# Linear result writes, gathers by batch and a deeper pipeline in the third expert layer of a four-layer attention and expert stack

## The chip, the cores and the metric

The kernel runs on one core of one Trainium2 chip. The metric is the time of one execution on the device, in microseconds (us), as the median of three runs. PE is the matrix engine (TensorE) and PEld its weight loads, DVE is VectorE, ACT is ScalarE, POOL is GpSimd, and SP is SyncE, which here only issues transfers and keeps them in order. HBM is the chip's memory off the core; SBUF and PSUM are the two memories on it.

## The reference, cut to what matters

`x` has 4 batches of 512 tokens of 128 numbers, `ctx` 4 batches of 154 tokens. Four layers follow each other, each with a cross-attention and a layer of 8 experts. The change lies in the experts of layer 2 (counted from 0, so the third) and in the attentions of layers 2 and 3:

```python
x = x + _L2_xattn_ref(_layernorm(x), ctx, ...)      # 16 heads of 64, softmax over 154 keys
x = x + _L2_ffn_ref(_layernorm(x), wg, w1, w2)
x = x + _L3_xattn_ref(_layernorm(x), ctx, ctx, ...) # 16 heads of 64
x = x + _L3_ffn_ref(_layernorm(x), ...)

def _L2_ffn_ref(x, wg, w1, w2):                     # w1 8x128x256, w2 8x256x128
    gate_logits = xt @ wg
    top_vals, top_idx = jax.lax.top_k(gate_logits, TOP_K)          # TOP_K = 2
    weights = jax.nn.softmax(top_vals, axis=-1)
    combine = zeros((T, E)).at[arange(T)[:, None], top_idx].add(weights)
    h = jax.nn.gelu(jnp.einsum('td,edf->etf', xt, w1), approximate=False)
    y = jnp.einsum('etf,efd->etd', h, w2)
    out = jnp.einsum('te,etd->td', combine, y)
```

Every token goes to two experts, so each expert layer has 4096 rows to compute, and a token's result is the sum of two weighted rows.

## The kernel before

**Experts of layers 2 and 3 (`region`).** POOL scatters the 4096 normalised rows, each with its weight and its target, by indirect DMA into `xq_d` in HBM, so that the rows of an expert stand together (`slot_q` holds the place of every row, `scatter_rows`, L903). The rows are then worked in NRUN = 23 runs, 16 of 256 rows and 7 of 128, which make 39 blocks of 128 rows. Per run SP loads the expert's two weight matrices (`weights(k)`, L721 and L722, into one of NQ = 4 slots) and SP or ACT loads the rows (`rows(k)`, L730 and L1269, into one of 8 slots). PE turns the rows (`columns`, L2857), ACT copies them (`xc_q`), PE makes the hidden layer (`hidden`, L2869), ACT applies the gelu, PE multiplies by the second matrix (`down`, L2882), and DVE scales each row by its gate weight into one of NY = 6 result tiles `yq` (`weigh`, L2030). PE's order is hidden(k+1), columns(k+2), down(k). DVE also works out for each block where its rows belong (`targets`, L2022), and POOL scatters the block to those rows of `yq_d` in HBM by indirect DMA (L922), 39 times. When all have landed, SP issues eight linear loads (L756) of the two halves into `acc` and `y_other`. DVE adds them to `x_tok` (L1778, L1780).

**Attentions of layers 2 and 3.** The heads are taken in 4 groups of 4, and the work in 16 stages, one for a group and a batch. A stage has 8 steps m, one for a pair of heads and a tile of 128 tokens: PE makes the scores (L2777 to L2779), DVE their maxima (L2278), ACT the exponentials (L1323), DVE the reciprocal of the sum, POOL scales (`normalise`, L1085 and L1086), and PE turns the result and multiplies by the values one stage later. A group has 13 preparations (`prep`: products of the weights with the context, copied by ACT and DVE). Those of groups 0 and 1 stand ahead of stage 0, those of group 2 in stages 4 to 7, of group 3 in stages 8 to 11. The order of stages is written out in `ORDER`: group 0 for batches 0 to 3, then group 1 for batches 0 to 3, then a mix. Before a batch's first stage its layer norm has to be ready: DVE adds the results to `x_tok` and takes the statistics (L1728, L1731, L1736), POOL raises to the power -1/2 (`rstd`, L892), DVE normalises (L1745), PE turns (`turned_x`), ACT copies, and POOL takes the low part of the split (`low_x`, L1071). In the order before, DVE does batches 0 and 1 and most of batch 2 ahead of its first maxima.

The engines run each its own list in order; semaphores tie them. The name of a loop's step is the order of the code: nothing is scheduled by a planner except the positions in tables such as `ORDER`.

Of the kernel before, what the change touches and what calls it, by code (L numbers as in the profile page):

```python
# [6 lines left out]
def xattn_moe_stack(nc, t, out):  # L7
# [55 lines left out]
    NQ, NX, NY = 4, 8, 6  # L63
# [9 lines left out]
    PRIOR = (None, None, 7, 8)  # L73
    SPOT = (0, 2, 3, 4, 5, 6, 7, 8, 9, 10, 11, 12, 13)
# [4 lines left out]
    BEHIND = {(0, "A"): [("x", 1)], (0, "C"): [("x", 2)], (2, "A"): [("x", 3)], (13, "A"): [("f", 0)], (14, "A"): [("f", 1)], (14, "D"): [("t", 0)], (15, "A"): [("lg", 0)], (15, "D"): [("t", 1)]}  # L79
# [8 lines left out]
    def ring(l):  # L88
# [70 lines left out]
    with ExitStack() as ctx:  # L159
# [229 lines left out]
        w1_q = [over(f"w1_q{u}", [P, 4 * P], F32, w_q_at[u])[0] for u in range(NQ)]  # L389
        w2_q = [over(f"w2_q{u}", [P, 4, D], F32, w_q_at[u] + 2048)[0] for u in range(NQ)]  # L390
        xq = [over(f"xq{u}", [P, HALVES, XC], F32, q_at + 1056 * u)[0] for u in range(NX)]
        yq = [over(f"yq{u}", [P, HALVES, D], F32, pt_at + 10240 + 1024 * u)[0] for u in range(NY)]
        xc_q = [over(f"xc_q{u}", [P, RUN], F32, pt_at + 8192 + 1024 * u)[0] for u in range(2)]
        h_q = [over(f"h_q{u}", [P, 4, RUN], F32, pt_at + 4096 * u)[0] for u in range(2)]
# [259 lines left out]
        def _(sp):  # L654
# [56 lines left out]
            def region(l):  # L711
# [3 lines left out]
                def weights(k):  # L715
# [3 lines left out]
                    if k >= NQ:  # L719
                        sp.wait_ge(q_yp, run(l, k - NQ) + 1)  # L720
# [2937 lines left out]
```

## Time and profile before

| | |
|---|---|
| median of three runs | 1168.32 us (1166.42, 1168.32, 1173.46) |
| profiled execution, first to last instruction | 1219.8 us |
| mean granted clock of PE in it | 0.930 of full speed |
| busy: PE, DVE, ACT, POOL | 86%, 59%, 53%, 47% |
| third expert layer, first turn of rows to SP's first result load | 784.9 to 853.2 us |
| first scores of the attentions of layers 2 and 3 | 528.3 and 872.0 us |

The profiled execution has no time of its own other than its span, which is 51.5 us longer than the median. So the places in the trace tell what waits for what, and a time that is read off it may be up to some per cent longer than in the runs that are timed. A line number such as L922 is one of the kernel before.

### The profile page before, as it was taken

To read this page: it belongs to the slowest core of one execution; us is meant where nothing else is said; L and a number is where in the kernel's file an instruction comes from. 1 tells how busy PE (TensorE), PEld (TensorE's weight loads), DVE (VectorE), ACT (ScalarE), POOL (GpSimd) and SP (SyncE) were. 2 spreads that over 40 slices of the span, in tenths; PEclk is the share of its full clock that TensorE was granted. 3 is DMA by queue.
4 is the path that set the end of the run, shared out by engine and by line. 5 is a ranking of instruction groups with operands and counts; after the bars stand their busy time and mean duration, and the time that the engine had idled before them with its cause. 6 is when DMAs were issued, how large, how long until landed. Compare 5 with 4: busy or idle time off the path is not lost.

```text
span 1219.8 us, 22199 instructions
## 1 busy us (share of the span) xinstructions
PE 1054.1 (86%) x6815; PEld 797.4 (65%) x6815; DVE 717.3 (59%) x2444; ACT 643.9 (53%) x2117; POOL 571.5 (47%) x926
## 2 busy tenths in 40 slices
PE   4988999758889998979999987777799999977994
PEld 3865788735555667856767665566566776654994
DVE  5575354476776771386767784322876776852444
ACT  2244323357778723358778862222387888731321
POOL 5223655451000152566555656366375555655452
PEclk9987999989999988889999997697899999986997
DMA  2003556599600124110000001364300000014665
GB/s 63 13 27 112 161 165 208 163 156 385 237 1 1 36 68 137 54 30 19 1 19 19 1 5 43 85 187 121 87 19 1 2 1 1 2 33 129 200 208 173
DMA packets 116005, 102.87 MB, mean 84 GB/s; under 512 B 18027, under 2 KB 97571, under 8 KB 115888
## 3 DMA queue, kind: packets, MB, share of 16 engines
q1 hardware_dynamic: 105280, 82.71, 23.3%
q0 software_dynamic: 8448, 17.20, 4.2%
q10 hardware_dynamic: 2160, 1.53, 0.5%
q8 instruction: 57, 0.93, 0.3%
q14 instruction: 60, 0.49, 0.1%
HBM read 65.04 MB, written 36.36 MB: 83 GB/s over the span
## 4 chain that ended last, share of the span: by engine, by line
PE 61%; DVE 16%; issue 6%; ACT 5%; POOL 4%; DMA 4%; another core or an unknown queue 3%; SPq 2%; DVEq 0%; ACTq 0%; POOLq 0%
PE ps L2973 4%; PE ps L2777 4%; PE ps L2869 4%; PE ps L2882 4%; PE ps L2779 4%; PE ps L2778 4%; PE ps L2987 3%; PE ps L3515 3%; PE ps L3519 3%; PE ps L3168 2%; PE ps L3528 2%; PE ps L3001 2%; PE ps L3327 2%; ACT ex L1323 2%
## 5 line engine op out<-in xcount | busy, mean ns | idle before, releaser
L1323 ACT ACTIVATE ex<-ps,nmx 128x154 f32<-128x154 f32 x512 | 194.0, 391 | 75.0 <-DVE nmx L2278 73.2
L1085 POOL TENSOR_TENSOR pp<-ex,rc 128x256 f32<-128x256 f32 x256 | 157.6, 615 | 146.0 <-DVE rc L2283 145.0
L2278 DVE TENSOR_REDUCE nmx<-ps 128x2 f32<-128x308 f32 x256 | 119.6, 470 | 60.2 <-PE ps L2779 59.2
L922 POOL DMA_INDIRECT yq_d<-yq,ids_q x78 | 74.7, 957 | 79.4 <-DVE yq L2030 60.6
L2973 PEld LDWEIGHTS ps<-ident,pp 128*128 128x128 f32 x640 | 73.9, 142 | 55.5 <-POOL pp L1086 46.5
L2777 PE MATMUL ps<-kp,q_s 128*128 128x308 f32 x256 | 95.5, 373 | 15.1 <-ACT ex L1323 12.6
L1323 ACT ACTIVATION_READ_ACCUMULATOR ex<-ps,nmx 128x1 f32 x512 | 105.2, 205 | 0.0
L2973 PE MATMUL ps<-ident,pp 128*128 128x128 f32 x640 | 100.1, 280 | 2.8 <-POOL pp L1086 2.8
L1440 ACT ACTIVATE pe<-ps,nmx 128x154 f32<-128x154 f32 x256 | 84.9, 394 | 32.0 <-DVE nmx L2161 30.9
L892 POOL TENSOR_TENSOR ln_r<-ln_v,mhalf 128x4 f32<-128x4 f32 x32 | 32.7, 1021 | 105.4 <-DVE ln_v L1736 86.8
L2869 PE MATMUL ps<-xc_q,w_q 128*128 128x256 f32 (+1 forms) x276 | 63.6, 371 | 19.3 <-issue 11.5
L2778 PE MATMUL ps<-kp,q_s 128*128 128x308 f32 x256 | 79.1, 309 | 0.0
L2779 PE MATMUL ps<-kp,q_s 128*128 128x308 f32 x256 | 79.0, 309 | 0.0
L2609 DVE SCALAR_TENSOR_TENSOR h_r<-ps,bias_r,g_r 128x256 f32<-128x256 f32 (+1 forms) x92 | 34.6, 437 | 73.7 <-ACT g_r L1598 45.2
L903 POOL DMA_INDIRECT xq_d<-xe,slot_q x64 | 61.8, 965 | 33.0 <-issue 17.9
L2752 PE MATMUL ps<-ident_bf 128*128 128x512 bf16 x193 | 66.7, 497 | 6.1 <-DVE ln_v L1736 6.1
L2161 DVE TENSOR_REDUCE nmx<-ps 128x2 f32<-128x308 f32 x128 | 58.6, 474 | 21.6 <-PE ps L3155 21.2
L1086 POOL TENSOR_TENSOR pp<-ex,rc 128x52 f32<-128x52 f32 x256 | 70.9, 277 | 0.0
L2987 PE MATMUL ps<-pt_s,vv 128*64 128x512 f32 x256 | 69.0, 618 | 1.4 <-ACT pt_s L1336 1.4
L1241 ACT ACTIVATE xc_q<-ps 128x256 f32<-128x256 f32 (+1 forms) x46 | 16.0, 351 | 101.6 <-PE ps L2857 73.7
L2030 DVE TENSOR_SCALAR yq<-ps,xq 128x128 f32<-128x128 f32 x78 | 24.3, 347 | 74.9 <-PE ps L2882 48.9
L1130 POOL COPY pr<-pe 128x416 f32<-128x416 f32 x16 | 8.6, 537 | 123.7 <-ACT pe L1440 123.7
(481 smaller groups left out, 2831.6 us busy)
## 6 DMA issues: line engine op xcount, KB each, us to landing
w_r<-in_L_ffn_W SPq DMA_DIRECT2D x69, 256.0 KB
xq_d<-blankq SPq DMA_DIRECT2D x4, 4160.0 KB, 23.8
w_q<-in_L_ffn_W SPq DMA_DIRECT2D x46, 256.0 KB
w_q<-in_L_ffn_w SPq DMA_DIRECT2D x46, 128.0 KB
xq<-xq_d SPq DMA_DIRECT2D x24, 130.0 KB
w_s<-in_L_ffn_W SPq DMA_DIRECT2D x8, 256.0 KB
w_e<-in_L_ffn_W SPq DMA_DIRECT2D x8, 256.0 KB, 5.2
acc<-yq_d SPq DMA_DIRECT2D x8, 256.0 KB, 4.6
```

The source lines that it names most:

```text
L922: pool.indirect_dma_start(yq_d[:, :], bass.IndirectOffsetOnAxis(ap=ids_q[:, c:c + 1], axis=0), yq[k % NY][:, h, :], None).then_inc(q_out[k ...
L1085: pool.tensor_tensor(pp[st % 2][:, m % 4, 2 * j:2 * j + 2, :], w[:, :, 0:P], r.broadcast_to([P, 2, P]), ALU.mult)
L1086: pool.tensor_tensor(pp[st % 2][:, m % 4, 4, :].rearrange("p (h c) -> p h c", h=4)[:, 2 * j:2 * j + 2, 0:SK - P], w[:, :, P:SK], r.broadca ...
L1323: ins = act.activation(ex[:, tt % NEX, j, :], ps[:, tt % 3, j * SK:(j + 1) * SK], ACT.Exp, bias=nmx8[:, tt % 8, j:j + 1], accum_out=sm8[:, ...
L1440: ins = act.activation(pe1[st % 2][:, m % 4, m // 4 * 2 + j, 0:SK], ps[:, tt % 3, j * SK:(j + 1) * SK], ACT.Exp, bias=nmx8[:, tt % 8, j:j ...
L2278: dve.tensor_reduce(nmx8[:, tt % 8, :], ps[:, tt % 3, 0:2 * SK].rearrange("p (h s) -> p h s", h=2), AX.X, ALU.max, negate=True).then_inc(n ...
L2777: mm(bank, w[0], x[0], start=first, stop=False)
L2778: mm(bank, w[0], x[1], start=False, stop=False)
L2779: return mm(bank, w[1], x[0], start=False, stop=last)
L2869: last = mm(ps[:, k % 2 * 2 + c // 2, c % 2 * RUN:c % 2 * RUN + P * TALL[k]], w1_q[k % NQ][:, c * P:(c + 1) * P], xc_q[k % 2][:, 0:P * TAL ...
L2973: last = pe.transpose(ps[:, bank, k * P:(k + 1) * P], pp[st % 2][:, k, c, :], ident[:, :])
L2987: last = mm(ps[64 * i:64 * i + 64, 5 + j, :], vv[g % 2][:, b, 64 * h:64 * h + 64], pt_s[h][:, :], start=True, stop=False)
```

## The change

**Results.** In layer 2, POOL's 39 scatters, DVE's `targets` and the eight loads at the end are gone. SP writes each run's results as they stand, with one linear DMA (`results(k)`), to a new tensor `yl_d`, at the row where the run stands in `xq_d` (`row_y`, two small DVE operations in the table of runs). In SP's order `results(k-4)` stands behind `weights(k)`, and waits for DVE's `weigh(k-4)`. `yl_d` is filled with zeros beforehand, by two more DMAs behind the zero writes of `xq_d` in layer 1.

**Gathers.** Within the attention of layer 3 POOL gathers, with `slot_q`, the two rows of each token from `yl_d` into `acc` and `y_other`: `fetch(b, i)`, 32 indirect DMAs of 128 rows, 8 for a batch. Twelve stand ahead of the first `rstd`, two between it and `low_x(0)`, four behind that, and 14 among the 32 `normalise` of stages 0 to 3.

**Pipeline.** In layer 2 there are three hidden and three result banks instead of two, four `xc` tiles instead of two, and PE's order is hidden(k+2), columns(k+4), down(k). Weights have six slots instead of four.

**Order of the attentions of layers 2 and 3.** Groups 0 and 1 go batch by batch: (0, b0), (1, b0), (0, b1), (1, b1) and so on. Layer norm and turning of batches 1 to 3 move into stages 0 to 5, and the 26 preparations of groups 2 and 3 to stages 2 to 12. Ahead of stage 0 only batch 0 is left. In layer 3, twelve instead of eight preparations of group 1 stand ahead of batch 0's sums.

```diff
+    PREP_AT = {(2, 0): [(2, 0)], (2, 2): [(2, 1)], (3, 0): [(2, 4)], (3, 1): [(2, 5)], (3, 3): [(2, 6)], (4, 0): [(2, 7)], (5, 0): [(3, 0)],
...
-    ORDER = [(g, b) for g in range(2) for b in range(B)] + [(2, 0), (2, 1), (3, 0), (3, 1), (2, 2), (3, 2), (2, 3), (3, 3)]
+    ORDER = [(g, b) for b in range(B) for g in range(2)] + [(2, 0), (2, 1), (3, 0), (3, 1), (2, 2), (3, 2), (2, 3), (3, 3)]
...
+    FETCH_AT = {(0, 1): (2, 2), (0, 3): (2, 3), (0, 5): (2, 4), (0, 6): (2, 5), (1, 1): (2, 6), (1, 3): (2, 7), (1, 5): (3, 0), (2, 1): (3, 1), (2, 3): (3, 2),
+                (2, 5): (3, 3), (2, 6): (3, 4), (3, 1): (3, 5), (3, 3): (3, 6), (3, 5): (3, 7)}
...
+                def results(k):
+
+                    sp.wait_ge(q_y, max(run(l, k), 1))
+                    r = sp.value_load(row_y[0:1, UNIT[k]:UNIT[k] + 1])
+                    sp.wait_ge(q_y, run(l, k) + 1)
+                    sp.dma_start(yl_d[bass.ds(r, P * TALL[k]), :].rearrange("(p h) c -> p h c", h=TALL[k]), yq[k % NY][:, 0:TALL[k], :]).then_inc(q_lin[k % NY], 16)
...
-                for k in range(NQ, NRUN):
+                for k in range(4, NRUN):
                     weights(k)
...
+                    if l == 2:
+                        results(k - 4)
+                if l == 2:
+                    for k in range(NRUN - 4, NRUN):
+                        results(k)
+                    return
...
+                for h in range(2):
+                    sp.dma_start(yl_d[h * EMPTY // 2:(h + 1) * EMPTY // 2, :].rearrange("(k p) c -> p k c", p=P),
+                                 blankq[:, 0:1, 0:D].broadcast_to([P, EMPTY // (2 * P), D])).then_inc(q_init, 16)
...
-                for k in range(NRUN):
+                for k in range(NRUN if l == 3 else 0):
                     pool.wait_ge(q_y, run(l, k) + 1)
...
+                def fetch(b, i):
+
+                    c, n = i % 2, i // 2
+                    into = (acc, y_other)[c]
+                    pool.indirect_dma_start(into[:, b * S + n * D:b * S + (n + 1) * D], None, yl_d[0:EMPTY, :],
+                                            bass.IndirectOffsetOnAxis(ap=slot_q[:, b, c * TB + n:c * TB + n + 1], axis=0)).then_inc(y_row[b], 16)
...
+                if l == 3:
+                    for k in range(NRUN - NY, NRUN):
+                        pool.wait_ge(*sent(2, k))
+                    for i in range(2 * TB):
+                        fetch(0, i)
+                    for i in range(4):
+                        fetch(1, i)
                 rstd(2 * l, 0)
-                rstd(2 * l, 1)
...
                 for k in range(NRUN):
-                    if k + 1 < NRUN:
-                        hidden(k + 1)
-                    if k + 2 < NRUN:
-                        columns(k + 2)
+                    if k + ahead < NRUN:
+                        hidden(k + ahead)
+                    if k + 2 * ahead < NRUN:
+                        columns(k + 2 * ahead)
                     down(k)
```

SP's list in the third expert layer, in mid loop. Before, behind the last rows that SP loads, only weights are left (`w_q` are weight slots):

```order
245 L730 ISA
246 L730 DMA xq_213<-xq_d 128x260
247 L718 TENSOR_LOAD expert_q
248 L721 ISA
249 L721 DMA w_q_200<-in_L_ffn_w 128x256
250 L722 DMA w_q_204<-in_L_ffn_w 128x2x128
251 L718 TENSOR_LOAD expert_q
```

Now a result write stands between the weights of two runs (`w_h` are weight slots, `ids_q` holds `row_y`, `yq` are result tiles):

```order
244 L739 TENSOR_LOAD expert_q
245 L742 ISA
246 L742 DMA w_h_203<-in_L_ffn_w 128x256
247 L743 DMA w_h_213<-in_L_ffn_w 128x2x128
248 L748 TENSOR_LOAD row_q
249 L751 ISA
250 L751 DMA xq_225<-xq_d 128x260
251 L756 TENSOR_LOAD ids_q
252 L758 ISA
253 L758 DMA yl_d<-yq_227 128x256
254 L739 TENSOR_LOAD expert_q
```

Every load of weights behind the first five has moved to behind a write that waits for DVE.

POOL's list at the head of the fourth attention, before, from the last two scatters (`wo_hl` are parts of the output weights, `ln_r` is `rstd`, `q_s` is `low_x`, `pp` is `normalise`):

```order
488 L922 DMA yq_d<-yq_217,ids_q 9984x128
489 L922 DMA yq_d<-yq_218,ids_q 9984x128
490 L1024 TENSOR_TENSOR wo_hl_86<-w_raw,ones 128x256
491 L1026 TENSOR_TENSOR wo_hl_87<-w_raw,wo_hl_86 128x256
492 L892 TENSOR_TENSOR ln_r<-ln_v,mhalf 128x4 x2
493 L1071 TENSOR_TENSOR q_s<-xnT,q_s 128x512
494 L892 TENSOR_TENSOR ln_r<-ln_v,mhalf 128x4
495 L1085 TENSOR_TENSOR pp_90<-ex,rc 128x256
```

Now, from the twelfth gather on:

```order
481 L1114 DMA y_other<-yl_d,slot_q 128x128
482 L929 TENSOR_TENSOR ln_r<-ln_v,mhalf 128x4
483 L1114 DMA acc<-yl_d,slot_q 128x128
484 L1114 DMA y_other<-yl_d,slot_q 128x128
485 L1108 TENSOR_TENSOR q_s<-xnT,q_s 128x512
486 L1114 DMA acc<-yl_d,slot_q 128x128
487 L1114 DMA y_other<-yl_d,slot_q 128x128
488 L1114 DMA acc<-yl_d,slot_q 128x128
489 L1114 DMA y_other<-yl_d,slot_q 128x128
490 L1129 TENSOR_TENSOR pp_90<-ex,rc 128x256
```

The gathers stand ahead of and between the steps that lead to the first scores and the first `normalise`; the `rstd` of later batches have gone from there.

DVE's list at the same place, before, from batch 0's `rstd` result on to the first maxima `nmx` (`xn_tok` is the normalised batch, `kp` and `vr` are preparations):

```order
1176 L1745 TENSOR_SCALAR xn_tok<-x_tok,ln_mv,ln_r 128x128 x4
1177 L1778 TENSOR_TENSOR x_tok<-x_tok,y_other 128x512
1178 L1780 TENSOR_TENSOR x_tok<-x_tok,acc 128x512
1179 L1728 BN_STATS ln_st<-x_tok 128x6 x4
1180 L1731 BN_AGGR ln_mv<-ln_st 128x2 x4
1181 L1736 TENSOR_SCALAR ln_v<-ln_mv 128x4
1182 L1852 TENSOR_TENSOR kp_79<-ps,kp_78 128x308 x2
```

Now:

```order
1155 L1800 TENSOR_SCALAR xn_tok<-x_tok,ln_mv,ln_r 128x128 x4
1156 L1914 COPY vr_94<-ps 128x256
1157 L2344 TENSOR_REDUCE nmx<-ps 128x2 x2
1158 L2349 RECIPROCAL rc<-sm 128x2
1159 L1826 TENSOR_TENSOR x_tok<-x_tok,y_other 128x512
1160 L2344 TENSOR_REDUCE nmx<-ps 128x2
```

The sums and statistics of batches 1 and 2 have moved behind the first maxima, where the add (L1826) waits for batch 1's gathers.

## Rows read from the trace of the kernel before

**Rows 1.** The page, part 4: the chain that ended last, by engine.

```profile
PE 61%; DVE 16%; issue 6%; ACT 5%; POOL 4%; DMA 4%; another core or an unknown queue 3%; SPq 2%; DVEq 0%; ACTq 0%; POOLq 0%
```

**Rows 2.** Stretches: length, busy PE, PEld, DVE, ACT, POOL, clock, DMA share, GB/s.

```profile
330.00:390.00 60.00, 56.13 (x446) 35.20 (x446) 41.82 (x93) 48.16 (x133) 3.23 (x6) 1.00 0.01 2
528.30:573.40 45.10, 39.98 (x232) 28.02 (x233) 32.84 (x107) 36.30 (x148) 33.35 (x69) 0.92 0.05 13
872.00:919.00 47.00, 39.77 (x231) 27.02 (x232) 35.68 (x109) 35.21 (x148) 33.78 (x69) 0.96 0.04 13
919.00:970.00 51.00, 50.21 (x348) 36.96 (x346) 35.68 (x99) 41.03 (x161) 28.46 (x68) 1.00 0.01 2
```

**Rows 3.** Line L922 in 784.9 to 852.9; its engine's idle time (us, times).

```profile
L922 POOL DMA_INDIRECT yq_d<-yq,ids_q x39: 952/958/961, 792.0 to 850.8; - x39
...
  issue: 9.9, 31
```

**Rows 4.** Waits, 785 to 850: who, for whom, us, times, longest.

```profile
ACT xc_q L1241 <- remote: 20.2, 6, 4.8
...
DVE yq L2030 <- remote: 15.1, 4, 4.5
```

**Rows 5.** Timeline in the third expert layer: start, us, engine, line, operation.

```profile
797.80 0.33 SPq L721 DMA_DIRECT2D w_q<-in_L_ffn_w  x1
...
799.09 0.33 SPq L721 DMA_DIRECT2D w_q<-in_L_ffn_w  x1
...
800.74 0.61 DVE L2030 TENSOR_SCALAR yq<-ps,xq 128x128 f32<-128x128 f32 x2 [1.79 <-issue]
...
802.58 1.06 PE L2882 MATMUL ps<-w_q,h_q 128*128 128x128 f32 x8
...
803.48 1.03 PE L2869 MATMUL ps<-xc_q,w_q 128*128 128x256 f32 x4
...
804.34 0.38 PE L2857 MATMUL ps<-ident,xq 128*128 128x128 f32 x2
...
804.56 0.61 PE L2882 MATMUL ps<-w_q,h_q 128*128 128x128 f32 x4
```

**Rows 6.** The chain that ended last, 790 to 815: start, us, what.

```profile
798.23 3.12 DMA w_q<-in_L_ffn_w
...
807.65 2.38 DMA w_q<-in_L_ffn_w
```

**Rows 7.** Line L968, the first layer's gathers: ns min/median/max, starts.

```profile
L968 POOL DMA_INDIRECT xr<-xr_d,src_i x39: 940/961/1124, 108.1 to 220.6; - x39
```

**Rows 8.** Timeline from the last scatter to the fourth attention.

```profile
853.16 0.38 SPq L756 DMA_DIRECT2D acc<-yq_d  x1
...
861.17 0.68 DVE L1778 TENSOR_TENSOR x_tok<-x_tok,y_other 128x512 f32<-128x512 f32 x1
...
864.19 1.04 POOL L892 TENSOR_TENSOR ln_r<-ln_v,mhalf 128x4 f32<-128x4 f32 x1 [10.98 <-DVE ln_v L1736]
...
869.43 1.01 POOL L892 TENSOR_TENSOR ln_r<-ln_v,mhalf 128x4 f32<-128x4 f32 x1 [4.21 <-DVE ln_v L1736]
...
870.41 1.46 POOL L1071 TENSOR_TENSOR q_s<-xnT,q_s 128x512 fp32r<-128x512 f32 x1
...
871.97 0.38 PE L2777 MATMUL ps<-kp,q_s 128*128 128x308 f32 x1 [0.70 <-issue]
...
876.97 0.63 POOL L1085 TENSOR_TENSOR pp<-ex,rc 128x256 f32<-128x256 f32 x1 [0.46 <-DVE rc L2283]
```

**Rows 9.** POOL's groups in 872 to 919: busy us, mean ns, idle before.

```profile
L1085 POOL TENSOR_TENSOR pp<-ex,rc 128x256 f32<-128x256 f32 x31 | 19.5, 629 | 9.4 <-DVE rc L2283 9.4
L1086 POOL TENSOR_TENSOR pp<-ex,rc 128x52 f32<-128x52 f32 x31 | 8.9, 286 | 0.0
```

**Rows 10.** The page, part 6: zero writes, KB each, us to landing.

```profile
xq_d<-blankq SPq DMA_DIRECT2D x4, 4160.0 KB, 23.8
```

More of the change, by code:

```diff
@@ L93, in spot @@
             def spot(k):
-                return [("prep", st // B + 1, SPOT.index(4 * (st % B) + k))] if B <= st < NST - B and 4 * (st % B) + k in SPOT else []
+                return [("prep", g, i) for g, i in PREP_AT.get((st, k), [])]
             def behind(at):
@@ L1269, in rows @@
                     act.dma_start(xq[u][:, 0:TALL[k], :], xq_d[l - 2][bass.ds(r, P * TALL[k]), :].rearrange("(p h) c -> p h c", h=TALL[k])).then_inc(q_x[u], 16)
-                columns(0)
-                columns(1)
-                for k in range(NRUN):
-                    first_half(k)
-                    if l == 2 and NX <= k + NQ + 2 < NRUN:
-                        rows(k + NQ + 2)
-                    if k + 2 < NRUN:
-                        columns(k + 2)
+                ahead = AHEAD_OF[l]
+                for k in range(2 * ahead):
+                    columns(k)
+                for k in range(ahead - 1):
+                    first_half(k)
+                for k in range(NRUN):
+                    if k + ahead - 1 < NRUN:
+                        first_half(k + ahead - 1)
+                    if l == 2 and NX <= k + 6 < NRUN:
+                        rows(k + 6)
+                    if k + 2 * ahead < NRUN:
+                        columns(k + 2 * ahead)
                 if l == 3:
@@ L1311, in step_prep @@
                 def step_prep(st, k):
-                    if B <= st < NST - B and 4 * (st % B) + k in SPOT:
-                        prep(l, st // B + 1, SPOT.index(4 * (st % B) + k))
+                    for g, i in PREP_AT.get((st, k), []):
+                        prep(l, g, i)
                 def exps(st, m):
@@ L2268, in step_prep @@
                 def step_prep(st, k):
-                    if B <= st < NST - B and 4 * (st % B) + k in SPOT:
-                        prep(l, st // B + 1, SPOT.index(4 * (st % B) + k))
+                    for g, i in PREP_AT.get((st, k), []):
+                        prep(l, g, i)
                 def maxima(st, m):
@@ L2851, in columns @@
                 def columns(k):
-                    pe.wait_ge(*landed(q_x, l, k, 16))
+                    pe.wait_ge(*rows_in(l, k))
                     if k >= 2:
@@ L2888, in region @@
                 idle_products(2, 0 if l == 2 else 16)
-                columns(0)
-                columns(1)
-                hidden(0)
+                ahead = AHEAD_OF[l]
+                for k in range(2 * ahead):
+                    columns(k)
+                for k in range(ahead):
+                    hidden(k)
                 for k in range(NRUN):
-                    if k + 1 < NRUN:
-                        hidden(k + 1)
-                    if k + 2 < NRUN:
-                        columns(k + 2)
+                    if k + ahead < NRUN:
+                        hidden(k + ahead)
+                    if k + 2 * ahead < NRUN:
+                        columns(k + 2 * ahead)
                     down(k)
@@ L2945, in step_prep @@
                 def step_prep(st, k):
-                    if B <= st < NST - B and 4 * (st % B) + k in SPOT:
-                        prep(l, st // B + 1, SPOT.index(4 * (st % B) + k))
+                    for g, i in PREP_AT.get((st, k), []):
+                        prep(l, g, i)
                 def scores(st, m):
```

207 lines of the change are left out of this document (111 added, 96 removed), and 3 rows, old and new, of the table PREP_AT.

## The prediction

> **What bounds the kernel now.** I read the page first. The chain that ended last is 61% PE, and 3% of it, some 37 us, is a releaser that the profile can't name [rows 1]. Then I cut the trace into stretches. In stages 4 to 7 of the fourth attention PE is busy for 50.21 of 51.00 us; in stages 0 to 3 for 39.77 of 47.00, and in stages 0 to 3 of the third attention for 39.98 of 45.10 [rows 2]. So the attentions are PE's, and only their beginnings have something to give: 5 to 7 us each. In the third expert layer POOL sets the pace: 39 scatters of 0.958 us, each with 9.9/31 = 0.32 us of issue ahead of it, the first at 792.0, the last at 850.8 [rows 3]. Back to back they would take 39 x 1.27 = 49.5 us; they take 59.8. The other 10 us are stalls in which ACT and DVE wait for a "remote" releaser, 20.2 and 15.1 us side by side [rows 4]: PE had finished, and the signal was seen late, while POOL was issuing indirect transfers.
>
> The profiled span, 1219.8 us, is 51.5 us over the median. The nameless releaser's 37 us are of that size, and I take it as likelier than not (about two in three) that most of these stalls belong to the profiled execution alone. So I make each sum twice where it matters, with the stalls as in the span and without.
>
> **The third expert layer.** Removed: 39 scatters, 23 small DVE `targets` and eight loads. Call T the moment at which all results are in HBM. Before, SP's first load starts at 853.16 [rows 8], so T = 853.2; without the stalls 792.0 + 49.5 + 1.4 (what lies between the last scatter's end, 850.8 + 0.96, and 853.16) = 842.9.
>
> After, the pace is a loop through SP. SP's list is `weights(k)`, `results(k-4)`, `weights(k+1)`: the six slots don't help past the first five, since the load for run k+5 stands behind the write of run k, which waits for DVE's `weigh(k)`. The loop, for runs of 256 rows: write issued 0.4 (an issue is 0.33, with its gap), weights issued 799.09 - 797.80 = 1.29 [rows 5], landing 2.38 to 3.12 [rows 6], hidden 804.34 - 803.48 = 0.86, columns 804.56 - 804.34 = 0.22, down 803.48 - 802.58 = 0.90, `weigh` 0.61 [rows 5], and four hand-overs of about 0.1: 7.1 to 7.8 us. hidden(k+5) stands ahead of down(k+3), so a loop spans three runs: 2.4 to 2.6 us a run. PE alone would need 0.86 + 0.22 + 0.90 = 1.98, SP alone 1.29 + about 0.87 for a write with its register load (estimated from the same rows: a load, an issue) = 2.16, POOL before 2 x 1.27 = 2.54. So the loop is the bound, and hardly shorter than POOL's step. The first `weigh` comes 1.3 us later than before (0.86 + 2 x 0.22 more on PE ahead of the first down), at about 792.7; 15 steps of 2.46 give 829.6; the seven runs of 128 rows take about 1.6 each, because SP has no weights left for the last of them: 841; then an issue of 0.4 and a landing that the trace doesn't show, for which I take 2.4 to 3.1 of the weight loads: T = 844, 840 to 848 with the ends of the landings. Against 853.2 that is 9 us saved, against 842.9 it is 1 us lost. Weighted toward the second: **-2 us, from -9 to +5**.
>
> A page of the Trainium skill speaks against the whole move: "DMA: Bandwidth & Descriptors", section "Issuing engines are not separate DMA queues", has it that starting transfers from another engine only saves sequencer time, which is usually small beside the transfer. The trace differs for POOL, whose issue is 1.27 us a block and fills 49.5 of 59.8 us [rows 3], so by the rule this term would be 0 and by the rows it is down to -9.
>
> **The head of the fourth attention and its first four stages.** Before, the eight loads, DVE's sums and statistics lead to the first `rstd` at 864.19 = T + 11.0, `low_x(0)` at 870.41 behind `rstd` of batch 1, first scores 871.97 = T + 18.8, first `normalise` 876.97 = T + 23.8 [rows 8]. After, POOL has to issue 12 gathers first. Their price is that of the nearest rows, the first layer's gathers, 0.961 us [rows 7], with the same issue gap 1.27: the first `rstd` is at T + 15.2 or later. DVE is ready at about the same time: eight gathers 10.2, a landing of 2.4 to 3.1, sums and statistics 864.19 - 861.17 = 3.0 give T + 15.6 to 16.3. So `rstd` comes 4.5 us later. Back come 1.0 us, because `low_x(0)` no longer stands behind the second `rstd` (869.43, which had waited 4.21 us for DVE) [rows 8]. Two gathers lie in the wait for `low_x`; four stand behind it: low_x ends 6.7 us after `rstd` starts, plus 4 x 1.27 = 11.8, where before `normalise` came 12.8 us after it. POOL thus enters stage 0 about 3.5 us later than before, counted from T.
>
> From there POOL has in stages 0 to 3: 32 `normalise` of 0.629 + 0.286, overlapping to 0.88 [rows 9] = 28.2; 14 gathers 17.8; two `rstd` 2.1; two `low_x` 2.9; the split of output weights 1.3: 52.3 us. PE had these stages in 47.0 [rows 2]. POOL becomes the bound of these stages and ends them 5.3 us later, 8.8 in all. Two things come off. PE takes the last results of a stage only in the middle of the next one, a quarter of 11.8 us, from which it can live once, 2 to 3 us. And five of the 26 preparations now lie in stages 2 and 3, under that wait; by PE's time of stages 4 to 7 against 0 to 3, (50.21 - 39.77) / 13 = 0.8 us each with part of it the fuller pipeline, 0.6 each, that is 3 us less later on. 8.8 - 2.5 - 3 = 3.3; DVE's add of batch 1 waits in stage 0 for gathers 13 to 16, which takes away some of the earlier first maxima: 1. **+4.5 us, from 0** (gathers that fit into POOL's idle 13 us) **to +10** (no slack, nothing regained).
>
> **The third attention.** The same new order, without gathers. `low_x(0)` loses the `rstd` ahead of it, 1.0; DVE no longer does batches 1 and 2 ahead of the first maxima; PE's idle time in stages 0 to 3 is 45.10 - 39.98 = 5.1 [rows 2], of which the pipeline's filling stays. What is moved, sums and statistics of three batches, lands in stages where DVE is busy for 32.84 of 45.10 us and PE is the bound. **-3 us, from -5 to 0.**
>
> **At nothing.** The zeros of `yl_d`, 2 x 4.2 MB behind those of `xq_d`: a write of that size landed in 23.8 us [rows 10], two in up to 48. They are hidden by layer 1's attention, in which the DMA engines are at 0.01 for the 60 us from 330 to 390 [rows 2]; without that cover they would cost up to 48. POOL's wait for them stands ahead of the scatters of layer 2, behind a whole attention. Two DVE operations for `row_y`: 0.3 us in a stretch in which POOL scatters. Three banks instead of two: no instruction. SP's eight loads were last in their queue ahead of weights for groups 2 and 3, which now start earlier.
>
> **Sum.** -2 + 4.5 - 3 = -0.5: **1168 us**, no change. In the profiled execution it would be -9 + 4.5 - 3 = -7.5, a span of about 1212. A measurement of this kernel can't tell less than about 1% (12 us) from no change.
>
> **The rivals.** *The stalls are in the timed runs as well and leave with the scatters.* For it: they stand where POOL issues indirect transfers back to back [rows 3, 4]. Against it: the span is 51.5 us too long, and something must account for that. Then the region gives -9, the third attention -3, and if the gathers in stages 0 to 3 find POOL idle, 0 in the head: -12, **1156 us**.
>
> *POOL's queue in the fourth attention decides (slower).* The 32 gathers that stood nowhere before are 32 x 1.27 = 40.6 us on the engine that has 33.78 of 47.00 busy already in stages 0 to 3 [rows 2]. From T to the end of stage 3 POOL then has 15.2 + 11.8 + 52.3 = 79 us, where PE came there in 18.8 + 47.0 = 66. As soon as less than 3 of those 13 us is regained, the head costs 10; with the loop at 2.6 us and T at 848 (+5), and 2 from the third attention: +13, **1181 us**. For it: POOL's rows leave no gap that isn't counted. Against: the middle of the next stage as slack, and the preparations already done.
>
> *The move does nothing in the expert layer,* because the loop through SP is as long as POOL's step (2.54 against 2.4 to 2.6) and what the stalls took is taken by the wait for weights: 0 + 4.5 - 3 = +1.5, **1170 us**. The section of the Trainium skill named above would give this time too.
>
> **How the numbers follow.** Forecast 0.38, stalls 0.30, POOL's queue 0.22, nothing moved 0.10. Of the stalls' case 0.25 lies beyond 1%, of POOL's 0.20; of the forecast's own spread (-8 to +9 or so, past the bounds -14 to +15 of the three terms hardly ever) 0.04 lies below and 0.05 above. That gives faster 0.29, same 0.46, slower 0.25. The range leaves out a tenth at each end: 1151 to 1182; the forecast's own range is 1160 to 1177.
>
> **What would show it.** In the new trace: runs of the third expert layer 2.4 to 2.6 us apart, with SP's weight loads issued right behind result writes and PE waiting for `w_h`; no "remote" waits in the region; POOL without a gap over 1 us from the first gather to the end of stage 3, and PE waiting there for `pp`; first scores about 21 us behind the last result's landing. Wrong would make it: runs 2 us apart (PE the bound), gathers that take less than 1.2 us of POOL, or a stall behind the twelve gathers that holds back DVE's preparations.

## The result

The changed kernel takes 1218.1 us, median of four runs (1216.2 to 1220.62); the kernel before, timed beside it, 1170.12. The ratio is 1.0406 [1.0376, 1.0436]: **4% slower**, above the predicted range. The profiled execution has a span of 1216.6 us and a time of 1218.55, so this trace stands for the timed runs.

The trace of before did not. The kernel before, profiled once more (run e1_before_again), has a span of 1164.2 us and a time of 1165.91. Its trace has no wait on "remote" and no nameless releaser in its chain, so [rows 1] and [rows 4] showed something that belonged to one execution. From here on the trace after is read against this second one.

The page of the kernel after, part 1 (PE's busy time alone) and part 4:

```profile
PE 1056.8 (87%) x6815; PEld 800.5 (66%) x6815; DVE 714.4 (59%) x2423; ACT 647.2 (53%) x2117; POOL 569.3 (47%) x919
...
PE 58%; DVE 13%; POOL 8%; DMA 6%; issue 6%; ACT 4%; SPq 3%; POOLq 0%; DVEq 0%; ACTq 0%
```

The same two lines of the kernel before, second profile:

```profile
PE 1032.1 (89%) x6815; PEld 781.7 (67%) x6815; DVE 717.8 (62%) x2444; ACT 644.2 (55%) x2117; POOL 572.8 (49%) x926
...
PE 60%; DVE 15%; POOL 7%; issue 6%; DMA 6%; ACT 5%; SPq 2%; DVEq 0%; POOLq 0%; ACTq 0%
```

The change cost 52.4 us of span. PE has the same 6815 instructions, and they take 24.7 us longer; the other 27.7 us are PE's idle time. Both have to be found. Cut at the first and last exponentials of the two attentions, at the first `columns` and the last `weigh` of the third expert layer, the stretches of after are these (columns as in [rows 2]: start and end, length, PE, PEld, DVE, ACT, POOL busy, granted clock, DMA share, GB/s):

```profile
520.80:727.80 207.00, 188.19 (x1195) 134.09 (x1195) 145.37 (x466) 155.94 (x619) 121.09 (x270) 0.96 0.03 9
...
774.30:832.20 57.90, 44.77 (x288) 38.63 (x289) 11.93 (x39) 19.17 (x47) 2.31 (x3) 0.97 0.60 172
832.20:859.50 27.30, 17.02 (x104) 12.64 (x105) 12.17 (x33) 6.38 (x15) 17.91 (x19) 0.81 0.23 63
859.50:1070.10 210.60, 189.24 (x1195) 135.81 (x1194) 144.89 (x447) 155.61 (x619) 137.51 (x286) 0.94 0.03 9
1070.10:1216.60 146.50, 123.27 (x787) 102.45 (x786) 65.02 (x268) 38.89 (x104) 71.27 (x76) 0.87 0.53 155
```

And those of the kernel before, second profile:

```profile
521.20:712.80 191.60, 183.27 (x1189) 130.97 (x1190) 140.43 (x442) 154.85 (x619) 118.67 (x269) 0.98 0.03 10
...
759.20:806.90 47.70, 42.30 (x291) 37.52 (x291) 13.39 (x61) 19.39 (x48) 33.52 (x36) 1.00 0.70 205
806.90:834.50 27.60, 18.17 (x105) 13.16 (x105) 19.33 (x59) 6.00 (x15) 10.02 (x11) 0.81 0.38 110
834.50:1025.70 191.20, 182.51 (x1189) 130.07 (x1190) 138.96 (x421) 154.23 (x619) 119.02 (x269) 0.99 0.01 4
1025.70:1164.20 138.50, 116.84 (x787) 97.99 (x786) 64.91 (x268) 38.81 (x104) 71.12 (x76) 0.92 0.56 164
```

The two attentions lost 15.4 and 19.4 us, the third expert layer 10.2, the stretch from its last result to the first exponential nothing (27.3 against 27.6), and the rest behind the fourth attention 8. Ahead of the third attention and between it and the expert layer the lengths are the same (520.8 against 521.2; 46.5 against 46.4). In each attention PE is busy for 5 to 7 us more, at a lower granted clock, and idle for 10 to 13 us more. So 11.6 of the 24.7 us of busy time lie in the attentions; 6.4 lie in the tail and 5.2 ahead of the third attention, in work that the change left as it was.

**Where the attentions stall.** The timeline of after, from DVE's variances of batch 1 in stage 0 of the third attention to PE's `turned_x` of that batch (start, us, engine, line, operation; in brackets the idle time ahead and what ended it):

```profile
527.99 0.41 DVE L2417 TENSOR_SCALAR ln_v<-ln_mv 128x4 f32<-128x4 f32 x1
...
529.72 1.01 POOL L929 TENSOR_TENSOR ln_r<-ln_v,mhalf 128x4 f32<-128x4 f32 x1
...
530.77 0.60 DVE L2401 TENSOR_SCALAR xn_tok<-x_tok,ln_mv,ln_r 128x128 f32<-128x128 f32 x2 [1.34 <-POOL ln_r L929]
...
531.75 0.88 DVE L2401 TENSOR_SCALAR xn_tok<-x_tok,ln_mv,ln_r 128x128 f32<-128x128 f32 x2
...
532.77 1.09 PE L3087 MATMUL ps<-ident,xn_tok 128*128 128x128 f32 x4 [4.57 <-DVE xn_tok L2401]
```

PE ran dry for 4.57 us. `turned_x(1)` stands in PE's list behind the second scores of stage 1, and it needs a chain that begins only at the end of stage 0: `ln_v` behind step 7, `rstd` behind POOL's last `normalise` of the stage, and two halves of the normalising on DVE, which stand behind the first and the second maxima of stage 1. Everything behind it on PE, the scores of the same stage among it, waits too. The waits of after from 500 to 1080 (who, for whom, us, times, longest) have this six times, once for each of batches 1 to 3 in each attention:

```profile
PE ps L3087 <- DVE xn_tok L2401: 26.1, 6, 6.3
```

The waits have a second price. The stretches of 2 us around the wait shown above (528.2 to 532.77), of after:

```profile
526.00:528.00 2.00, 1.81 (x15) 1.54 (x13) 1.46 (x11) 1.61 (x10) 1.71 (x5) 1.00 0.00 0
528.00:530.00 2.00, 0.20 (x2) 0.00 (x0) 1.43 (x4) 1.72 (x9) 1.68 (x5) 1.00 0.00 0
530.00:532.00 2.00, 0.00 (x0) 0.00 (x0) 1.23 (x6) 0.21 (x1) 0.83 (x2) 0.99 0.00 0
532.00:534.00 2.00, 1.23 (x6) 1.26 (x7) 0.62 (x2) 0.75 (x5) 0.77 (x2) 0.50 0.00 0
534.00:536.00 2.00, 2.00 (x10) 1.83 (x8) 0.55 (x2) 2.00 (x7) 0.70 (x2) 0.50 0.00 0
536.00:538.00 2.00, 2.00 (x5) 0.29 (x4) 0.55 (x2) 1.42 (x6) 0.98 (x3) 0.50 0.00 0
538.00:540.00 2.00, 2.00 (x15) 1.91 (x14) 0.90 (x2) 0.00 (x0) 0.00 (x0) 0.80 0.00 0
```

PE stands still, the granted clock falls from 1.00 to 0.50 (1.2 of 2.4 GHz) as the wait ends, and PE then works at 0.50 for some 6 us. Stretches at 0.50 follow all six waits of after; the 11.6 us of longer busy time in the two attentions go with them. The page "TensorE: Matmul & The Clock Gate" of the Trainium skill, section "HAM oscillation — how this bites in real kernels", warns of this with a kernel whose PE waits for DMA: idle gaps of PE bring the half clock, and the work behind them starts at it. The trace agrees, with waits for another engine.

**The third expert layer.** What stood at [rows 3] and [rows 5] is now the queue of SP. Its timeline (SP's issues):

```profile
787.55 0.36 SPq L758 DMA_DIRECT2D yl_d<-yq  x1
788.37 0.33 SPq L742 DMA_DIRECT2D w_h<-in_L_ffn_w  x1
...
789.67 0.36 SPq L758 DMA_DIRECT2D yl_d<-yq  x1
...
791.81 0.36 SPq L758 DMA_DIRECT2D yl_d<-yq  x1
...
795.38 0.36 SPq L758 DMA_DIRECT2D yl_d<-yq  x1
```

Weights are issued right behind a result write. Over 17 steps, from 784.39 to 826.24, the writes come 2.46 us apart, where the prediction had 2.4 to 2.6. PE waits for the weights, as the waits of after from 774 to 836 show:

```profile
PE ps L2931 <- DMA w_h<-in_L_ffn_w: 10.8, 10, 2.0
```

**The head of the fourth attention.** Timeline of after; it answers to [rows 8]:

```profile
835.75 1.01 POOL L1114 DMA_INDIRECT acc<-yl_d,slot_q  x1 [58.87 <-DMA yl_d<-yq]
...
850.67 1.05 POOL L929 TENSOR_TENSOR ln_r<-ln_v,mhalf 128x4 f32<-128x4 f32 x1
...
858.27 0.41 PE L2838 MATMUL ps<-kp,q_s 128*128 128x308 f32 x1
```

And of the kernel before, second profile:

```profile
815.93 0.38 SPq L756 DMA_DIRECT2D acc<-yq_d  x1
...
822.78 1.04 POOL L892 TENSOR_TENSOR ln_r<-ln_v,mhalf 128x4 f32<-128x4 f32 x1 [8.24 <-DVE ln_v L1736]
...
830.56 0.38 PE L2777 MATMUL ps<-kp,q_s 128*128 128x308 f32 x1 [0.29 <-issue]
```

From the moment T at which the results are in HBM to the first `rstd` it is 14.9 us, before 6.9 (in [rows 8] it had been 11.0). But the last result is in HBM sooner: 835.75 - 832.1 = 3.7 us behind the start of the last `weigh`, before 815.93 - 806.9 = 9.0.

POOL does have gaps of over 1 us behind the first gathers, while it waits for DVE; the longest in stage 1 is 2.53 us:

```profile
878.90 0.61 POOL L1129 TENSOR_TENSOR pp<-ex,rc 128x256 f32<-128x256 f32 x1 [2.53 <-DVE rc L2349]
```

### The profile page after: what moved, and what is told of

Read it like the earlier page. It is cut to its first block, busy times and chain, and to the rows that moved or that the text cites. A ratio compares the mean times of both kernels' runs of the same rounds, so it can differ in the third digit from the quotient of the medians.

```text
span 1216.6 us, 22265 instructions
## 1 busy us (share of the span) xinstructions
PE 1056.8 (87%) x6815; PEld 800.5 (66%) x6815; DVE 714.4 (59%) x2423; ACT 647.2 (53%) x2117; POOL 569.3 (47%) x919
## 4 chain that ended last, share of the span: by engine, by line
PE 58%; DVE 13%; POOL 8%; DMA 6%; issue 6%; ACT 4%; SPq 3%; POOLq 0%; DVEq 0%; ACTq 0%
PE ps L3037 5%; PE ps L3051 4%; PE ps L2838 4%; PE ps L2840 4%; PE ps L2839 4%; PE ps L2931 4%; PE ps L2944 3%; PE ps L3228 2%; PE ps L3575 2%; PE ps L3579 2%; PE ps L3065 2%; PE ps L3588 2%; PE ps L3387 2%; POOL pp L1129 2%; PE ps L2813 2%
## 5 line engine op out<-in xcount | busy, mean ns | idle before, releaser
L3037 PEld LDWEIGHTS ps<-ident,pp 128*128 128x128 f32 x640 | 77.2, 146 | 56.4 <-POOL pp L1130 43.7
L3037 PE MATMUL ps<-ident,pp 128*128 128x128 f32 x640 | 103.3, 287 | 2.3 <-POOL pp L1130 2.0
L2838 PE MATMUL ps<-kp,q_s 128*128 128x308 f32 x256 | 97.3, 380 | 7.8 <-ACT ex L1382 7.4
L2839 PE MATMUL ps<-kp,q_s 128*128 128x308 f32 x256 | 80.9, 316 | 0.0
L2840 PE MATMUL ps<-kp,q_s 128*128 128x308 f32 x256 | 80.7, 315 | 0.0
L2670 DVE SCALAR_TENSOR_TENSOR h_r<-ps,bias_r,g_r 128x256 f32<-128x256 f32 (+1 forms) x92 | 34.6, 437 | 69.2 <-ACT g_r L1653 58.8
L1130 POOL TENSOR_TENSOR pp<-ex,rc 128x52 f32<-128x52 f32 x256 | 73.6, 287 | 0.0
L3051 PE MATMUL ps<-pt_s,vv 128*64 128x512 f32 x256 | 71.9, 641 | 1.4 <-ACT pt_s L1395 1.4
L2813 PE MATMUL ps<-ident_bf 128*128 128x512 bf16 x193 | 64.1, 481 | 6.2 <-DVE ln_v L1791 6.2
L2096 DVE TENSOR_SCALAR yq<-ps,xq 128x128 f32<-128x128 f32 x78 | 24.4, 347 | 66.5 <-PE ps L2944 66.3
L1395 ACT ACTIVATE pt_s<-ps 128x512 f32<-128x512 f32 x96 | 57.9, 603 | 8.9 <-PE ps L3037 8.9
L2838 PEld LDWEIGHTS ps<-kp,q_s 128*128 128x128 f32 x256 | 50.7, 198 | 13.8 <-ACT ex L1382 11.6
L959 POOL DMA_INDIRECT yq_d<-yq,ids_q x39 | 37.4, 958 | 43.7 <-DVE yq L2096 37.9
```

The costliest lines, as they stand in the source:

```text
L1130: pool.tensor_tensor(pp[st % 2][:, m % 4, 4, :].rearrange("p (h c) -> p h c", h=4)[:, 2 * j:2 * j + 2, 0:SK - P], w[:, :, P:SK], r.broadca ...
L2813: mm(ps[:, bank, :].rearrange("p (a c) -> p a c", a=4), ident_bf[:, :], ident_bf[:, :].rearrange("p (a c) -> p a c", a=1).broadcast_to([P, ...
L2838: mm(bank, w[0], x[0], start=first, stop=False)
L2839: mm(bank, w[0], x[1], start=False, stop=False)
L2840: return mm(bank, w[1], x[0], start=False, stop=last)
L3037: last = pe.transpose(ps[:, bank, k * P:(k + 1) * P], pp[st % 2][:, k, c, :], ident[:, :])
```

## The experiments

Theory at the start: the new order of the attentions costs, since `turned_x` stands on PE ahead of work that could go on; SP's loop costs a little; POOL's gathers a little more. Rivals: the gathers decide (the prediction's slower rival); the pipeline or the zeros decide; or the first profile's stalls hide a gain elsewhere.

All runs on one scale, from their traces. Att3 and att4 are first to last exponential of an attention; layer, first `columns` to last `weigh`; head, from there to the first exponential; tail, behind the fourth attention; waits, PE's for `turned_x` in both attentions (the row shown above). From the fourth column on the numbers are us; stretches run from start to start and hold to about 0.1 us.

| run | time, us | ratio to before | att3 | layer | head | att4 | tail | waits |
|---|---|---|---|---|---|---|---|---|
| e1, before | 1165.91 | (one run) | 191.6 | 47.7 | 27.6 | 191.2 | 138.4 | 0.6 |
| after | 1218.1 | 1.0406 | 207.0 | 57.9 | 27.4 | 210.6 | 146.5 | 26.1 |
| e8, after | 1215.13 | 1.0398 | 206.9 | 57.6 | 27.7 | 210.5 | 141.9 | 26.2 |
| e2, order alone | 1191.47 | 1.0213 | 206.3 | 47.8 | 24.0 | 204.7 | 140.2 | 21.8 |
| e9, e2 + half stage | 1179.11 | 1.0092 | 195.3 | 47.8 | 26.2 | 197.0 | 140.8 | 4.9 |
| e4, after, a stage earlier in layer 2 | 1203.65 | 1.0314 | 196.9 | 59.2 | 28.3 | 210.0 | 140.1 | 23.3 |
| e6, after + half stage | 1195.58 | 1.0223 | 194.7 | 58.8 | 26.9 | 201.3 | 142.7 | 7.6 |
| e5, after without 14 gathers | 1209.39 | 1.0361 | 206.7 | 57.9 | 27.3 | 204.9 | 139.5 | 21.1 |
| e7, results two later | 1203.62 | 1.0321 | 206.8 | 48.7 | 28.5 | 209.7 | 140.7 | 26.9 |
| e10, e6 + e7 | 1182.79 | 1.0119 | 194.6 | 48.5 | 27.0 | 201.1 | 140.8 | 6.1 |
| e12, pipeline alone | 1172.03 | 1.0036 | 191.3 | 50.4 | 26.9 | 191.2 | 137.6 | 0.7 |

**e1_before_again**: the kernel before, unchanged, profiled again.

> The kernel before, unchanged, profiled once more. If the 'remote' stalls of the first profile (ACT 20.2 and DVE 15.1 us in the third expert layer, others in the first) belong to that one execution: span within 1% of the median, 1160 to 1180 us, no 'remote' row, third expert layer from first columns to SP's first result load about 58 us instead of 68.3. If they belong to the kernel: span near 1220 us with the same rows.

Its span is 1164.2 us, with the scatters of the third expert layer undisturbed (line L922, its first and last start, and POOL's idle time ahead of it):

```profile
L922 POOL DMA_INDIRECT yq_d<-yq,ids_q x39: 954/958/961, 764.1 to 812.1; - x39
...
  issue: 11.0, 36
```

So 39 scatters take 48.0 us from first to last start, not the 58.8 of [rows 3]. The stalls that the writes were to take away are not there.

**e2_order_alone**: the kernel before with the new order of stages, of the layer norms and of the preparations, and nothing else of the change.

```diff
-    ORDER = [(g, b) for g in range(2) for b in range(B)] + [(2, 0), (2, 1), (3, 0), (3, 1), (2, 2), (3, 2), (2, 3), (3, 3)]
+    ORDER = [(g, b) for b in range(B) for g in range(2)] + [(2, 0), (2, 1), (3, 0), (3, 1), (2, 2), (3, 2), (2, 3), (3, 3)]
...
-                rstd(2 * l, 1)
...
-                    if st == 0:
-                        turned_x(1)
-                    elif st == 2:
-                        turned_x(3)
+                    if st in (1, 3, 5):
+                        turned_x((st + 1) // 2)
...
```

> The kernel before with the new order of both attentions alone (stages batch by batch, layer norm of batches 1 to 3 in stages 0 to 5, preparations in stages 2 to 12); results are scattered by POOL and loaded as before, old pipeline. Theory 1, a layer-norm chain in the new order stops PE three times in each attention (PE waits 4 to 5 us for xn_tok in stages 1, 3, 5): +22 to +28 us over before, 1190 to 1198. Theory 2, POOL's gathers in the fourth attention and the loop through SP make the loss: within 5 us of before, or a few us faster.

1191.47 us against 1167.06, ratio 1.0213 [1.0144, 1.0283]. The attentions are 14.7 and 13.5 us longer, and the head 3.6 shorter. The order alone is thus half of the loss, and the fourth attention has most of its loss without a single gather. PE's wait for `turned_x` in this kernel:

```profile
PE ps L3008 <- DVE xn_tok L2329: 21.8, 6, 4.6
```

**e4_stats_early_l2**: after, with the layer norms of batches 1 to 3 a whole stage earlier in layer 2 alone (batch 1 ahead of stage 0, batches 2 and 3 in stages 1 and 3).

```diff
+                if l == 2:
+                    rstd(2 * l, 1)
...
-                        if st in (0, 2, 4) and m == 7:
+                        if l == 3 and st in (0, 2, 4) and m == 7:
                             rstd(2 * l, st // 2 + 1)
+                        elif l == 2 and st in (1, 3) and m == 7:
+                            rstd(2 * l, (st + 3) // 2)
...
```

> The changed kernel, with the layer norm's statistics and rstd of batches 1 to 3 in the third attention (layer 2) one stage earlier than the change has them; all else of the change stays. Theory 1: stages 1, 3 and 5 of that attention fall from 16.5 to 18 us to about 12 to 14, 8 to 13 us less than the changed kernel, 1205 to 1210. Theory 2: no difference, 1216 to 1220.

1203.65 us, ratio 1.0314 [1.0237, 1.0390]. The third attention, which alone was changed, came back from 207.0 to 196.9; the fourth stayed at 210.0. Its stretch:

```profile
518.80:715.70 196.90, 182.66 (x1195) 130.32 (x1195) 142.97 (x456) 155.52 (x619) 118.60 (x269) 0.99 0.03 9
```

Of the 10.1 us, 5.5 are PE's busy time (188.19 to 182.66, at a granted clock of 0.99 for 0.96) and 4.6 its idle time, of which the waits for `turned_x` are 3.3 (11.7 us in three waits of after, 8.4 here). The 10.1 us are within the 8 to 13 that were expected, and the time is just under the 1205 to 1210. PE's busy time gave back more than the waits themselves: behind two of the three waits the granted clock stayed at 1.00, behind the third it fell to 0.50. But the waits only got shorter. The chain's first links now stand a whole stage earlier, and its last link holds PE all the same (waits of PE from 518 to 716, then the timeline of stage 1):

```profile
PE ps L3096 <- DVE xn_tok L2405: 8.4, 3, 3.5
...
525.54 0.94 DVE L2405 TENSOR_SCALAR xn_tok<-x_tok,ln_mv,ln_r 128x128 f32<-128x128 f32 x2
...
526.41 0.47 DVE L2348 TENSOR_REDUCE nmx<-ps 128x2 f32<-128x308 f32 x1
...
526.87 0.87 DVE L2405 TENSOR_SCALAR xn_tok<-x_tok,ln_mv,ln_r 128x128 f32<-128x128 f32 x2
...
527.89 0.63 PE L3096 MATMUL ps<-ident,xn_tok 128*128 128x128 f32 x4 [2.69 <-DVE xn_tok L2405]
```

DVE doesn't wait for `rstd` any more; it works through the maxima of stage 1, with a half of the normalising behind the first and one behind the second, while PE stands.

**e6_chain_half_stage**: after, with the chain half a stage earlier in both attentions: `rstd` behind step 3 instead of 7, sums and moments earlier on DVE, the first half of the normalising still in the stage before, the second behind the first maxima instead of the second.

```diff
-                        if st in (0, 2, 4) and m == 7:
+                        if st in (0, 2, 4) and m == 3:
                             rstd(2 * l, st // 2 + 1)
...
                     if begins:
-                        variances(begins)
+                        normed_half(begins, 0)
...
```

> The changed kernel, with the layer norm of batches 1 to 3 half a stage earlier in both attentions: sums, statistics and rstd end after steps 3 of stages 0, 2, 4 instead of 7, the first half of normalising stands at that stage's end; PE's list is unchanged. Theory 1 (six waits of PE for xn_tok, 26.1 us in the changed kernel's trace): they fall to under 8 us together, 18 to 24 us less than the changed kernel, 1193 to 1200. If PE is held by something else in these stages: less than 6 us.

1195.58 us, ratio 1.0223 [1.0164, 1.0281]. The attentions took 194.7 and 201.3 us, 12.3 and 9.3 less than after. PE's wait is down from 26.1 us to 7.6:

```profile
PE ps L3086 <- DVE xn_tok L2401: 7.6, 6, 2.1
```

In the third attention the granted clock is back at 1.00 and PE is busy for 181.61 us, where after had 0.96 and 188.19:

```profile
524.00:718.70 194.70, 181.61 (x1195) 129.22 (x1194) 145.03 (x467) 155.08 (x618) 120.16 (x270) 1.00 0.03 9
```

So more than half of what came back there (6.6 of 12.3 us) is PE's busy time, at the higher granted clock.

**e9_order_half_stage**: the same edit in e2, that is, without writes, gathers or pipeline.

> The kernel before with the new order of the attentions alone, and the layer norm of batches 1 to 3 half a stage earlier as in e6. Theory 1: nearly all of the 24 us of the order alone come back, 1165 to 1173, since both beginnings lose the work of batches 1 and 2. If the stages' order costs by itself (preparations spread over stages 2 to 12): 1180 or more.

1179.11 us, ratio 1.0092 [1.0053, 1.0131]. The attentions are 11.0 and 7.7 us shorter than in e2, with this wait:

```profile
PE ps L3007 <- DVE xn_tok L2329: 4.9, 6, 1.1
```

The time fell by 12.4 us of the 24.4 that the order costs, less than the 18.7 us of the attentions, of which the head gave up 2.2 again (26.2 for 24.0). So neither 1165 to 1173, "nearly all", came true, nor quite 1180 or more. In the attentions 3.7 and 5.8 us above the kernel before remain. What they are (the 4.9 us of waits that are left, the preparations in stages 2 to 12, the stages themselves) was not taken apart.

**e5_no_stage_gathers**: after without the 14 gathers in stages 0 to 3.

```diff
-                        if l == 3 and (st, m) in FETCH_AT:
-                            fetch(*FETCH_AT[st, m])
...
```

> The changed kernel without the 14 gathers in stages 0 to 3 of the fourth attention; batches 2 and 3 then add other data, so this part of the computation is left out. Theory 1: the stages lose only what they have over the third attention's, about 6 us: 1211 to 1213. Theory 2, POOL is the bound there: the 14 gathers are worth 14 x 1.27 = 18 us, 1200.

1209.39 us, ratio 1.0361 [1.0304, 1.0419]. The fourth attention is 5.7 us shorter, at 204.9, which is e2's 204.7. So these gathers cost 5.7 to 5.9 us, by two comparisons, and POOL's queue does not decide. PE's waits for `turned_x` are 5.0 us shorter (21.1 for 26.1): most of what the gathers cost, they cost by holding up the same chain. The time is a little under the 1211 to 1213 of the first theory.

**e7_results_two_later**: after, with SP's result write two runs later, `results(k-6)`.

```diff
-                    if l == 2:
-                        results(k - 4)
+                    if l == 2 and k >= 6:
+                        results(k - 6)
...
```

> The changed kernel, with results(k-6) instead of results(k-4) behind weights(k) in SP's list, so that no load of weights waits for DVE's newest rows. Theory of the loop through SP (write, weights, landing, hidden, down, weigh, over three runs): the pace falls from 2.46 us a run to SP's own 2.16, 4 to 7 us less than the changed kernel in the third expert layer. Rival, the landing of weights or SP's issue is the bound anyway: pace and time unchanged within 2 us.

1203.62 us, ratio 1.0321 [1.0264, 1.0378]. The layer's stretch falls from 57.9 to 48.7 us; the results come earlier and PE waits less for weights:

```profile
L2096 DVE TENSOR_SCALAR yq<-ps,xq x39: 340/350/352, 778.0 to 820.0; 128x128 f32<-128x128 f32 x39
...
PE ps L2931 <- DMA w_h<-in_L_ffn_w: 4.9, 7, 1.7
```

The place of the write in SP's list therefore costs 9 us, more than the 4 to 7 that were expected. The writes of the first 17 runs come 2.27 us apart (780.09 to 816.33; 2.16 was expected), and from the 17th write to the last it is 5.0 us, where after took 9.6. With the place moved, linear writes reach 48.7 us; POOL's scatters take 47.7 in e1 and 50.4 with the same pipeline (e12). T comes earlier:

```profile
823.66 1.01 POOL L1114 DMA_INDIRECT acc<-yl_d,slot_q  x1 [49.68 <-DMA yl_d<-yq]
```

That is 52.3 us behind the first `columns`, where it is 56.7 in e1 and 58.0 in e12.

**e12_pipeline_alone**: the kernel before with three hidden and result banks, four `xc` tiles, six weight slots and PE two runs deep in layer 2; POOL scatters as before.

> The kernel before with the pipeline alone: three banks, four xc tiles, order hidden(k+2), columns(k+4), down(k), six weight slots in layer 2; results scattered by POOL, old order of the attentions. POOL paces the third expert layer (39 scatters back to back, 1.263 us each), so no more than the later first scatter can be seen: 0 to +4 us against the kernel before, 1166 to 1171. If waits for PE or weights held the layer before: 3 to 8 us faster.

1172.03 us, ratio 1.0036 [1.0004, 1.0068]. The depth brings nothing while POOL sets the pace; its layer takes 50.4 us. The 4 us in time are at the upper end of the 0 to +4 that were expected.

**e10_chain_and_results**: after with the edits of e6 and e7 together.

> The changed kernel with both repairs, the layer norm half a stage earlier (as e6, 19.5 us less than the changed kernel) and results two runs later in SP's list (as e7, 11.5 us less). If the two losses are separate, they add: 1215 - 31 = 1184, some 17 us over the kernel before, for gathers, the later start of the third expert layer's pipeline and the order itself. If they hide each other: 1193 or more.

1182.79 us, ratio 1.0119 [1.0078, 1.0160]: the two repairs add up (against the 1215.13 us of e8, 19.6 and 11.5 alone, 32.3 together), and over two thirds of the loss are gone. Of the 17.5 us of span that are left against e1, 9.9 lie in the fourth attention and 3.0 in the third. No version that was tried beats the kernel before.

**e8_after_again**: after, unchanged.

> The changed kernel again, beside the others on the same chip. Its last expert layer took 8 us more than the kernel before's, with the same code: if that belongs to one execution, 138 to 141 us from the last exponential to the end and about 1210; if it belongs to the change, 146 us again and 1216 to 1220.

1215.13 us (1210.95 to 1217.29), ratio 1.0398 [1.0343, 1.0454]. The stretches in the table repeat those of after to 0.4 us, but for the tail, 141.9 against 146.5: neither of the two expected outcomes, but something between. The change leaves the work behind the fourth attention as it was, and that stretch was 137.6 to 146.5 us long; PE was busy in it for 116.84 us at a clock of 0.92 in e1 and 123.27 at 0.87 in after. What sets the clock there stays open.

## Why the prediction was wrong

**The step that failed** is that on the third attention: "What is moved, sums and statistics of three batches, lands in stages where DVE is busy for 32.84 of 45.10 us and PE is the bound", hence -3 us. It measured +15.4. I asked whether the engines had time for the moved work, and they had. I didn't ask when its result is needed. Ahead of the change, the layer norms of batches 1 and 2 were done early, and `turned_x` found them ready; after it, a chain over DVE, POOL and DVE ended too late for the place of `turned_x` in PE's list. The order of the code showed this before any run: `rstd` behind step 7 of stages 0, 2 and 4, the halves of the normalising behind the first two maxima of stages 1, 3 and 5, `turned_x` behind the second scores there. e6 and e9 moved that chain alone and took back 21.6 of 34.8 and 18.7 of 28.2 us in the two attentions, so the cause is shown for that part; what the rest of the order does stays open. Every link counts: with sums, statistics and `rstd` a whole stage earlier and the normalising left in place (e4), 8.4 of the third attention's 11.7 us of waits stayed. I also left out that PE works at a lower granted clock behind such waits: 4.9 and 6.7 us of PE's busy time in the two attentions. And of the 3 us that I took off, only 1.0 was worked out from rows.

**The head and the fourth attention's stages**, +4.5 with bounds 0 and +10, measured +19.1 (the head -0.3, the attention +19.4). The same error, 13.5 us by e2, stands in this term too. (The working adds up to 3.3 + 1 = 4.3, not 4.5, which changes nothing.) What the term was about, the gathers, is 5.7 to 5.9 us in the stages. In the head, T to the first scores is 22.5 us, where the prediction said about 21, but before it was 14.6 in the second profile and not 18.8. The head as a whole still costs nothing: counted from the last `weigh`, the gathers put the first `rstd` 8.0 us further behind T (14.9 for 6.9), T itself is 5.3 us closer (3.7 for 9.0), and the first exponential follows the first scores after 1.2 us instead of 3.9.

**The third expert layer**, -2 with bounds -9 and +5. The loop through SP was right, 2.46 us measured. T came 835.75 - 774.3 = 61.5 us behind the first `columns`, before 815.93 - 759.2 = 56.7, so +4.8: at the far end of the bounds, because the stalls that made the other end were one execution's. Two in three for that was too cautious, yet the right side. The rule of the Trainium skill that the prediction weighed ("DMA: Bandwidth & Descriptors", section "Issuing engines are not separate DMA queues": another issuing engine saves little) gives 0 for this term. For the length of the layer the traces agree: 48.7 us by SP in e7, 47.7 and 50.4 by POOL in e1 and e12. T itself came 4.4 us earlier by SP in e7 than in e1 (52.3 for 56.7), so with the write in a better place the move does save some time in this term. In the change the place in SP's list cost more than that, 9 us.

**At nothing.** This held, as far as the traces tell, for the zeros: the third attention's first exponential lies at 518.0 to 524.0 us in the seven traces with them and at 518.8 to 522.4 in the four later ones without. By e12 it held for the deeper pipeline.

**The rivals.** POOL's queue had the right sign and about 6 us of the loss, and its mark, no gap over 1 us up to the end of stage 3, did not appear (2.53 us in stage 1). The stalls' case is gone with e1: no later trace has them. The sum of the measured terms: 15.4 for the third attention, 19.4 for the fourth, 10.2 for the expert layer, -0.3 for the head, 8 for the tail, -0.3 elsewhere: 52.4 us, the difference of the spans. Of it 28.9 is the new order in the attentions (15.4, and 13.5 by e2; the layer norms' chain is the larger part of that), 9 SP's list and 6 the gathers; of the tail's 8, e8 shows only 3.5 again (141.9 against 138.4).

## What to carry to other kernels

When work is moved later because its engine has room, look up the consumer in the consumer's own list, follow the chain back to the moved work through each engine's list, and compare the place of every link, the last one too; a busy share says nothing on it. An instruction that waits for another engine (a result write in a queue of loads, a transpose among scores) holds everything behind it, and two runs or half a stage of distance were worth 9 and 20 us here. Where a profiled span differs from the timed runs by some per cent, profile once more before anything is counted from it.

## What was not expected of the hardware

One execution of the kernel before took about 55 us longer than the next one of the same program (spans 1219.8 and 1164.2), with waits on "remote" of up to 4.8 us in the third expert layer [rows 4], where POOL issued indirect transfers; none of the eleven other traces has such a wait. What they were stays open.

PE's 6815 instructions took 24.7 us longer in the trace of after than in e1's. 11.6 of it lie in the attentions, where PE worked at a granted clock of 0.50 for some 6 us after a wait of 4.57 us. 5.2 lie ahead of them, in a stretch that both kernels cross in 521 us (454.97 against 449.80 us busy, granted clock 0.94 against 0.95), and 6.4 in the tail; what lowered the clock there stays open.

Results land sooner by linear writes than by indirect ones. The median from issue to landing, of e1 from 760 to 820 and of after from 774 to 836 (256 rows a write, 128 rows a scatter):

```profile
yq_d<-yq,ids_q POOLq DMA_INDIRECT x39, 3.3
...
yl_d<-yq SPq DMA_DIRECT2D x16, 128.0 KB, 2.1
```

But the larger part of the difference at T (3.7 us instead of 9.0 behind the last `weigh`) is POOL's backlog: its last scatter starts at 812.1, 5.2 us behind the last `weigh`.
